# An attention and mixture-of-experts kernel: weighted values divided straight out of PSUM, gathers that add, a band mask moved to GpSimd for some steps

## What is computed

```python
xn = layernorm(x)
# attention: 32 heads of 8 channels; query i sees keys i-8 .. i+7
attn = (q @ k.T) * 8 ** -0.5
attn = where(m != 0, attn * m, -inf)      # m falls off with |i - j| / 16
s = softmax(attn) @ v @ proj_w.T + proj_b
# feed-forward: one of 8 experts per token (argmax of the router), and a shared expert
out[t] = (silu(xs @ gate_w[e]) * (xs @ up_w[e])) @ down_w[e]      # xs = xn * sigmoid(max logit)
shared = (silu(xn @ shared_gate_w) * (xn @ shared_up_w)) @ shared_down_w
g = silu(out + shared)
result = x + s * g
```

## Time and profile before

| | |
|---|---|
| Time before, median of 3 runs | 634.32 us (633.57 to 634.75) |
| The profiled execution's own time | 633.25 us |
| Its span in the profile | 631.4 us |
| TensorE busy | 557.1 us (88%) |
| VectorE busy | 403.7 us (64%) |
| ScalarE busy | 307.9 us (49%) |
| GpSimd busy | 187.0 us (30%) |

### The profile page before, as it was taken

The page is one execution under the profiler, slowest core; times in us unless marked ns, Lnnn a source line. Parts: engine busy times, 40 slices in busy tenths (PEclk is TensorE's granted clock), DMA queues, the critical chain, the costliest instruction groups (busy, mean ns, idle before and its releaser), DMA issues. The chain is left out here.

```text
span 631.4 us, 10599 instructions
## 1 busy us (share of the span) xinstructions
PE 557.1 (88%) x3358; PEld 479.0 (76%) x3358; DVE 403.7 (64%) x853; ACT 307.9 (49%) x762; POOL 187.0 (30%) x160
## 2 busy tenths in 40 slices
PE   1979999979889999999999999999886877769865
PEld 1757898758768999888999888898675655657754
DVE  6766556885756446456446456446688888886873
ACT  1473654458673644533634533645454533636331
POOL 6001011148861111000111000114655545532230
PEclk9989999979999999999999999999989899999997
DMA  8525441113327576576577566443133333331110
GB/s 292 180 70 174 151 141 55 49 49 99 113 92 216 163 223 202 167 203 199 143 218 208 168 203 190 126 129 115 50 110 110 108 99 101 117 102 26 35 42 17
DMA packets 107371, 82.89 MB, mean 131 GB/s; under 512 B 42293, under 2 KB 104757, under 8 KB 107317
## 3 DMA queue, kind: packets, MB, share of 16 engines
q1 hardware_dynamic: 98628, 68.72, 36.9%
q0 software_dynamic: 3072, 8.39, 4.2%
q10 hardware_dynamic: 5616, 5.11, 2.3%
HBM read 59.12 MB, written 23.07 MB: 130 GB/s over the span
## 5 line engine op out<-in xcount | busy, mean ns | idle before, releaser
L427 POOL TENSOR_TENSOR Sx<-Sx,mx 128x752 f32<-128x752 f32 x64 | 93.7, 1465 | 407.1 <-DVE mx L729 406.5
L945 PE MATMUL psV<-VB,PTs 128*128 128x132 f32 x1024 | 133.1, 282 | 30.2 <-ACT Or L470 29.7
L945 PEld LDWEIGHTS psV<-VB,PTs 128*128 128x128 f32 x1024 | 127.1, 193 | 36.1 <-issue 34.9
L470 ACT ACTIVATE Or<-psV 32x128 f32<-32x128 f32 x256 | 68.5, 268 | 150.5 <-DVE rs L759 146.2
L920 PE MATMUL psS<-kBD,qBD 128*128 128x188 f32 x512 | 104.0, 327 | 0.0
L920 PEld LDWEIGHTS psS<-kBD,qBD 128*128 128x128 f32 x512 | 86.9, 193 | 10.4 <-issue 2.2
L751 DVE STREAM_TRANSPOSE PTs<-Sx 128x512 f32<-128x512 f32 x128 | 82.9, 685 | 1.0 <-ACT Sx L500 1.0
L995 PE MATMUL psM<-xT,EB 128*128 128x128 f32 x624 | 76.4, 276 | 0.0
L995 PEld LDWEIGHTS psM<-xT,EB 128*128 128x128 f32 x624 | 73.8, 192 | 2.1 <-ACT qBD L489 1.3
L722 DVE TENSOR_TENSOR Sx<-psS,cst 128x752 f32<-128x752 f32 x64 | 59.6, 932 | 24.5 <-PE psS L920 24.5
L736 DVE SCALAR_TENSOR_TENSOR ea<-et,psM 128x256 f32<-128x256 f32 x39 | 16.4, 421 | 76.3 <-PE psM L995 47.2
(11 more groups left out here) (107 smaller groups left out, 689.3 us busy)
## 6 DMA issues: line engine op xcount, KB each, us to landing
EB<-in_L_ffn_gate_w SPq DMA_DIRECT2D x39, 256.0 KB, 2.9
EB<-in_L_ffn_up_w SPq DMA_DIRECT2D x39, 256.0 KB, 3.6
EB<-in_L_ffn_down_w SPq DMA_DIRECT2D x39, 256.0 KB, 3.1
VB<-v_dram SPq DMA_DIRECT2D x256, 32.0 KB
stage<-xs_dram SPq DMA_DIRECT2D x39, 128.0 KB, 2.2
ys_dram<-yb ACTq DMA_DIRECT2D x39, 128.0 KB, 3.1
xs_dram<-blank SPq DMA_DIRECT2D x9, 512.0 KB, 3.8
v_dram<-vS SPq DMA_DIRECT2D x8, 512.0 KB, 2.9
```

Source lines behind the costliest of these rows:

```text
L427: nc.gpsimd.tensor_tensor(s, s, mx[n % 3][:, :].unsqueeze(2).broadcast_to([P, 2 * G, KW]), ALU.subtract).then_inc(a_sub, 1)
L470: return nc.scalar.activation(dst, src, ACT.Copy)
L945: last = mm(psV[:, j, at:at + HS * VW], PTs[n % 2][:, k, j, i, :], VB[n % 2][:, i, k, :, VW * j:VW * j + VW], start=k == 0, stop=k == 1)
```

## The change

1. **Divide out of PSUM.** `o_out`, the tile Or and the semaphore `a_O` go. `divide(n)` becomes four VectorE instructions, one for each 32 partitions, that read psV and the reciprocals and write O. `weighted(n)` waits for `divide(n-1)` (`a_nrm`). `divide` and `turned` stand right after `invert`, ahead of the second expert tile and of the shared expert.
2. **Gathers that add.** `combine`, its semaphore `d_z` and the use of Y as landing buffer go. `gather(c)` is an indirect DMA with an add into the shared output's own rows. It is issued in the step before part c's silu, after `subtract` of that step, and first waits for the shared output (`f_sh`). ScalarE's `silu(c)` waits for the landing and, for part 3 on, for VectorE's silu three parts earlier.
3. **Masking on GpSimd.** In steps 0 to 7 and 18 to 37 (28 of 64), TensorE leaves out the two mask matmuls; GpSimd's new `banded(n)` adds the fp32 mask to Sx after `weigh(n)`, and `largest(n)` waits for it. In these steps `largest(n)` stands behind `normalise(n+1)` and `flipped(n-1)`. The constants that are loaded first grow by 12 x 47 columns (from 435 to 999 a partition).

```diff
+C_BAND = C_HEAD + HS
+C_STAY = C_BAND + 12 * KW
...
+def masked_late(n):
+    return n < BATCH or E0 <= n < E0 + NP
...
-        Or = sb("Or", [P, KC, 2, HS, HD])
...
+            def banded(n):
+                pool.wait_ge(a_mul, n + 1)
+                s = Sx[n % 3][:, :, :].rearrange("p (m r) k -> p m r k", r=HS)[:, :, :, 0:KW]
+                kind = 2 * KC * mask_kind(n)
+                nc.gpsimd.tensor_tensor(s, s, band[:, kind:kind + 2 * KC, :].unsqueeze(2).broadcast_to([P, 2 * KC, HS, KW]),
+                                        ALU.add).then_inc(a_add, 1)
...
             def gather(c):
...
-                if c >= 3:
-                    pool.wait_ge(d_w, c - 2)
+                pool.wait_ge(f_sh, c + 1)
                 for k in range(CT):
                     t = c * CT + k
-                    pool.indirect_dma_start(Y[b][:, k * C:(k + 1) * C], None, ys_dram,
-                                            bass.IndirectOffsetOnAxis(ap=slot[:, t:t + 1], axis=0)).then_inc(d_y[b], 16)
-
-            def combine(c):
...
-                nc.gpsimd.tensor_tensor(z, Y[b], z, ALU.add).then_inc(d_z, 1)
+                    pool.indirect_dma_start(shared_rows(c * CT)[:, k, :], None, ys_dram,
+                                            bass.IndirectOffsetOnAxis(ap=slot[:, t:t + 1], axis=0),
+                                            compute_op=ALU.add).then_inc(d_y[c % 3], 16)
 
             for n in range(LAST + 1):
-                for c in silu_at(n):
-                    combine(c)
                 if n < U:
+                    if masked_late(n):
+                        banded(n)
                     subtract(n)
...
-                if n == C_STEP:
-                    for c in range(3):
-                        gather(c)
-                for c in silu_at(n - 1):
-                    if c + 3 < NC:
-                        gather(c + 3)
+                for c in silu_at(n + 1):
+                    gather(c)
...
             def silu(c):
-                act.wait_ge(d_z, c + 1)
+                act.wait_ge(d_y[c % 3], 16 * CT * (c // 3 + 1))
+                if c >= 3:
+                    act.wait_ge(d_w, c - 2)
...
             def largest(n):
-                dve.wait_ge(a_mul, n + 1)
+                if masked_late(n):
+                    dve.wait_ge(a_add, len([k for k in range(n + 1) if masked_late(k)]))
+                else:
+                    dve.wait_ge(a_mul, n + 1)
...
             def divide(n):
                 dve.wait_ge(a_rec, n + 1)
-                dve.wait_ge(a_O, n + 1)
...
+                for h in range(HS):
+                    rows = slice(QB * h, QB * h + QB)
+                    last = tt(o[rows], v[rows, :, :, HD * h:HD * h + HD],
+                              inverse[rows].unsqueeze(3).broadcast_to([QB, KC, 8, HD]), ALU.mult)
+                last.then_inc(a_nrm, 1)
...
                 for j in range(KC):
-                    mm(psS[:, j, 0:BW], identb[:, :], maskb[:, kind:kind + 2, :, :].rearrange("p i r k -> p (i r k)"),
-                       start=True, stop=False)
+                    if not late:
+                        mm(psS[:, j, 0:BW], identb[:, :], maskb[:, kind:kind + 2, :, :].rearrange("p i r k -> p (i r k)"),
+                           start=True, stop=False)
```

More of the change, by code:

```diff
@@ L240, in build @@
         m_full = [sem(f"m_full{i}") for i in range(MB)]
-        a_qk, a_S, a_mul, a_max, a_sub, a_exp, a_PT, a_V, a_PV, a_O, a_rec, a_nrm, a_OT, a_s = (
-            sem("a_" + n) for n in ("qk", "S", "mul", "max", "sub", "exp", "PT", "V", "PV", "O", "rec", "nrm", "OT", "s"))
+        a_qk, a_S, a_mul, a_add, a_max, a_sub, a_exp, a_PT, a_V, a_PV, a_rec, a_nrm, a_OT, a_s = (
+            sem("a_" + n) for n in ("qk", "S", "mul", "add", "max", "sub", "exp", "PT", "V", "PV", "rec", "nrm", "OT", "s"))
         x_v, x_vd = ([sem(f"x_{n}{i}") for i in range(2)] for n in ("v", "vd"))
@@ L248, in build @@
         d_y, d_x, d_st = ([sem(f"d_{n}{i}") for i in range(3)] for n in ("y", "x", "st"))
-        d_z, d_t, d_w, d_g, d_o = (sem("d_" + n) for n in ("z", "t", "w", "g", "o"))
+        d_t, d_w, d_g, d_o = (sem("d_" + n) for n in ("t", "w", "g", "o"))
         x_tiles = x.rearrange("(t p) c -> p t c", p=P)
@@ L500, in exps @@
                 nc.scalar.activation(s, s, ACT.Exp).then_inc(a_exp, 1)
[L502 to L511, removed]
             def v_out(t):
@@ L763, in divide @@
                 dve.wait_ge(a_rec, n + 1)
[L764 removed]
                 if n >= 1:
                     dve.wait_ge(a_OT, n)
[L767 to L769 removed]
+                v = psV[:, :, 1:1 + 2 * HS * VW].rearrange("p j (i c) -> p j i c", c=VW)
+                inverse = rs[n % 2][:, :, :, :].rearrange("p j i s -> p j (i s)")
+                o = O[:, :, :, :, :].rearrange("p j i s d -> p j (i s) d")
+                for h in range(HS):
[3 more added lines that the diff above has]
+                last.then_inc(a_nrm, 1)
             def turned(n):
@@ L826, in _ @@
                     weigh(n)
-                    largest(n)
+                    if not masked_late(n):
+                        largest(n)
                 if n == 0:
@@ L842, in _ @@
                     flipped(n - 1)
+                if n < U and masked_late(n):
+                    largest(n)
                 for i in pair_at(n, 1)[:1]:
@@ L847, in _ @@
                     invert(n - 2)
+                    divide(n - 2)
+                    turned(n - 2)
                 for i in pair_at(n, 1)[1:]:
@@ L907, in scores @@
                 h, u = divmod(n, UH)
-                if n == 0:
+                late = masked_late(n)
+                if n == BATCH:
                     pe.wait_ge(s_cast, 2)
@@ L920, in scores @@
                         last = mm(psS[:, j, i * HS * KW:(i + 1) * HS * KW], qBD[h % 2][:, j, k, :, :].rearrange("p s q -> p (s q)"),
-                                  kBD[h % 2][:, j, :, k * QB:k * QB + KW], start=False, stop=i == 1)
+                                  kBD[h % 2][:, j, :, k * QB:k * QB + KW], start=late, stop=late or i == 1)
                 last.then_inc(a_S, 1)
@@ L939, in weighted @@
                 if n >= 1:
-                    pe.wait_ge(a_O, n)
+                    pe.wait_ge(a_nrm, n)
                 for j in range(KC):
```

13 lines of the change are left out of this document (2 added, 11 removed).

## The result

The changed kernel takes 614.76 us (612.71 to 615.40), against 634.27 for the kernel before: a ratio of 0.969, with an interval from 0.967 to 0.971. Forecast were 605 and a range of 594 to 618: faster, inside the range, 9.8 us slower than the likeliest case. The profiled execution took 614.93, its span 613.1.

What follows compares the result with a forecast made beforehand. TensorE was taken to bound steps 0 to 7 and 19 to 38, GpSimd's scatters 8 to 18, no single engine 41 to 54. 633.25 +1 -3 -0 -6.4 -0.7 -16 -2 -2 = 604.2, median 605, range 594 to 618.

Steps and rivals of the forecast that it cites:

- Constants: Before the first step: loading 564 more columns ahead of the weights costs 1 us (0 to 3.3).
- Steps 0 to 7: First stage: masks off TensorE save 2.6 us, with ScalarE's dropped `o_out` 3 in all (1 to 5).
- Steps 8 to 38: Scatters keep steps 8 to 18 unchanged; 20 masked steps in 18 to 37 save 0.32 us each, 6.4.
- `banded`: GpSimd's mask add takes 1.45 us; `largest` waits about 0.2 us for it, over 0.3 a step would be wrong.
- The divide: VectorE's four divides out of PSUM take 0.8 us together; a step with the hole before them gains 0.7.
- No combine: `result`'s first multiply falls to 0.68 us without GpSimd's `combine` beside it: 1.3 less in odd steps, 0.9 in even.
- Steps 41 to 54: VectorE needs 97 us, plus 0.55 a step for two near engines: 105 us, 16 less (10 to 24).
- Steps 55 to 62: Stage before the drain, TensorE near full: 2 us less (0 to 4).
- half the gain: Steps 41 to 54: divide costs 1.6 us or TensorE's bursts keep holes open, 8 of 16 lost; 615 us, chance 0.17.
- Masks don't pay: Masked stages: `banded` lengthens a chain TensorE awaits or collides with `normalise`, 9.4 us lost; 614 us, chance 0.10.
- all in balance: Steps 41 to 54 take 97 us instead of 105, first stage gains 5, steps 55 to 62 gain 3; 594 us, chance 0.12.
- The adding gather is slow: Steps 41 to 54: landings from 5.9 us after issue lengthen steps; at 12.1 us, 648 us in all; chance 0.06.

Runs made afterwards that it cites:

- early gathers: The changed kernel with the gathers of parts 0 to 11 issued two steps ahead of their silu instead of one: 604.45 us, ratio 0.953.
- silu last: The changed kernel with ScalarE's tanh of a part moved to the end of its step, gathers left where the change puts them: 604.49 us, ratio 0.953.

## Why the prediction came out as it did

The sign and the range held. In the terms of the profiled execution 604.2 were forecast and 614.93 came: of these 10.7 us, 5.6 lie in steps 41 to 54, 4.3 in steps 55 to 62, 1.9 in the drain and 0.4 in steps 39 and 40; the start gives 1.3 back (the rest is rounding and 0.1 from the other stages).

- **Constants.** Forecast +1, measured -0.3 (the first `weigh` at 27.21 instead of 27.53). 0.32 of this are the two mask matmuls that step 0 leaves out ahead of it, so the longer constants cost nothing that shows.
- **Steps 0 to 7.** Forecast -3, measured -2.8, of which the masks alone give 2.6.
- **Steps 8 to 38.** Forecast -6.4, all of it in steps 19 to 38; measured -6.7, but split otherwise: the windows give -2.4 for steps 8 to 18 (81.06 against 83.50) and -4.2 for 19 to 38 (227.80 against 232.02, forecast 225.6). In steps 20 to 37 most steps are 0.32 shorter, as forecast, and together they are 5.4 shorter (5.7 with the masks alone). Step 19 is 1.2 longer: the expert tiles start sooner and then wait for their weights, which no term held:

```profile
190.09 2.02 PE L996 MATMUL psM<-xT,EB 128*128 128x128 f32 x16 [1.63 <-DMA EB<-in_L_ffn_up_w]
```

For the 2.4 before it nothing was forecast; the divide alone gives 3.1 in steps 8 to 18 and loses 2.1 of it again in step 19, the masks alone give nothing there.
- **`banded`.** 1.68 us instead of 1.45. VectorE waited 11.7 us for it in 21 waits, 0.56 each where 0.2 was said and 0.3 was the sign of an error. That sign came up falsely: with the masks alone 8.9 us were gained, so the wait cost nothing that shows, as TensorE stayed full (226.96 of 227.80).
- **The divide.** Four of 0.287 and 1.19 together; the forecast was 0.8, and the term mis-sized is the overlap: 0.09 each was taken over from the reciprocals, and these four start 0.30 apart. The estimate of 1.03 by the Trainium skill, page VectorE: DVE Perf Modes, section The TRN2 errata, without overlap, was nearer, and still 0.16 low. From the reciprocals' end to the divide's end 1.23 us pass instead of 1.52 (in the drain 596.38 to 597.61): the hole went, and VectorE's own work filled most of it. A step with a hole gained 0.3 there and not 0.7. So VectorE's busy time came to 450.6 us and not to 425: the divides take 73.5 where the old ones took 23.5, 50 us more, and 64 x 0.5 = 32 had been said; another 7.6 are left open.
- **Steps 39 and 40, the drain.** Forecast -0.7 and -2, measured -0.3 and -0.1. In the drain the chain runs through psV, and psV is free no sooner: from the reciprocals' end of the drain's first pass TensorE restarts after 1.29 us before (614.61 to 615.90) and 1.37 after:

```profile
596.14 0.24 DVE L752 RECIPROCAL rs<-psV 128x8 f32<-128x8 f32 x2
596.42 1.19 DVE L764 TENSOR_TENSOR O<-psV,rs 32x128 f32<-32x128 f32 x4
...
597.75 3.67 PE L946 MATMUL psV<-VB,PTs 128*128 128x132 f32 x16 [6.96 <-DVE O L764]
```
- **No combine.** L804, the multiply that was L807, is 0.684 us in the mean over all 14, as forecast. The collision was GpSimd's `combine`: it is gone where only the gather is changed (0.683) and there where `combine` is kept (0.68 to 2.31 with the divide alone, 1.359 in the mean with the masks alone). The Trainium skill, page SBUF — State Buffer, section Who interferes with whom, agrees, for instructions of VectorE with two SBUF inputs beside one of GpSimd that reads SBUF; of those with one input it excepts the modes that use both of VectorE's ports, which the prediction left out. Step 45 takes 6.86 (forecast 6.4, and 6.8 with a divide of 1.19).
- **Steps 41 to 54.** Forecast -16 to 105, measured -10.4 to 110.7. **The step that failed** is in the adding gather: "`silu` on ScalarE now holds up what is queued behind it [...] those wait for TensorE work that ends later", and "hidden". The landing itself was sized rightly, 2 to 4 us behind the second issue (2.8 in the timeline of step 48, from 480.59). The issues were not: 1.55 to 2.01 us each on GpSimd where I had the gather's 0.95, so that they end 7.0 to 7.45 us after `weigh` and not 5.8, and ScalarE's tanh began mostly 1.3 to 3.5 us into the next step, not 0.9. And the q projections behind it had long been ready: the queue's order was not compared with when each piece of its work would be ready. That early gathers (same order, landings early up to step 52) and silu last (landings as late, other order) each bring 604.5 shows this to be the loss. The sign "no ScalarE wait of more than 1 us outside the last parts" failed as well: nine of the ten waits in steps 43 to 52 are 1.8 to 5.9 us long, though of these steps only 48 is longer than with early gathers. In steps 53 and 54, where the gather itself was held up, VectorE waits 2.64 and 2.30 us for the silu, and TensorE stands: for 3.02 us up to 532.13, after which the clock falls, and 16 matmuls take 3.86 us at a granted clock of 0.50.

```profile
535.79 3.86 PE L946 MATMUL psV<-VB,PTs 128*128 128x132 f32 x16 [0.99 <-DVE O L764]
537.70 0.63 ACT L546 ACTIVATE EB<-xnT 128x512 f32<-128x512 f32 x1 [5.91 <-DMA xnT<-ys_dram,slot]
538.37 0.69 DVE L797 SCALAR_TENSOR_TENSOR xnT<-EB,xnT 128x512 f32<-128x512 f32 x1 [2.30 <-ACT EB L546]
```

```profile
517.70:527.00 9.30, 7.67 (x49) 6.60 (x48) 8.24 (x20) 4.43 (x9) 4.57 (x3) 1.00 0.54 126
527.00:537.30 10.30, 6.29 (x32) 5.21 (x32) 6.70 (x14) 3.39 (x7) 4.58 (x3) 0.78 0.46 102
```
- **Steps 55 to 62.** Forecast -2, measured +2.3, +0.5 with early gathers, -0.5 with silu last. Step 62 has the wait for a landing again, 5.35 us, and takes 9.05 (before 7.56, with silu last 7.99). Step 56 takes 8.25 (before 7.48, with early gathers 6.57): TensorE's q projections ahead of it take 3.13 us, at a granted clock of 0.60, where early gathers show 1.89 at 1.00.

```profile
541.94 0.33 PE L917 MATMUL psS<-maskb,identb 128*128 128x376 bf16 x1 [2.29 <-DVE Sx L712]
...
543.99 3.13 PE L896 MATMUL psM<-xnT,wqkv 128*128 128x256 f32 x8
```

With the queue mended the kernel stands at 604.5, which is the 605 of the forecast, and partly by offset: VectorE's work was put 0.4 us a step too low (the divide), and the 0.55 us a step added for two engines near to each other was hardly needed.

Of the rivals, "half the gain" named 615 for another reason (a divide of 1.6 us, or open holes), so its number is no proof of it. "Masks don't pay" is out, since the masks alone give 8.9, and "all in balance" with its 97 us for steps 41 to 54. "The adding gather is slow" named a chain through the landing from 5.9 us on; the landings stay under it, and yet the gather alone makes the kernel 6.8 us slower, by the queue behind the wait and not by that chain.

The three parts alone give -4.3, +6.8 and -8.9 us, together -6.4; all at once they give -19.5. The missing 13 are the pairing of the first two, though no run has these two alone. The steps tell it: in steps 41 to 62 the parts alone give -1.0, +7.1 and 0, and all at once -8.1, so that the whole difference lies where the masks change nothing. The divide takes ScalarE's psV copies out from behind the wait (bringing them back cost 14.2 us, 11.4 of it in these steps), and the gather takes `combine` away, on which the divide's gain was spent. How the 13 divide between the two is not shown.

## What to carry to other kernels

When a transfer takes over an engine's work, write down who waits for its landing, and for each piece of work behind that wait the time at which it would have been ready: waits of up to 6.0 us at the end of a queue cost next to nothing here, and waits of up to 6.2 us in its middle cost 10 us in all. Ask too whether the next transfer needs something from behind the wait. An edit that only moves work from a second engine to the bounding one, as the divide does, gains by what it unties: price it together with the other edits of its queue, not as a hole closed. Do not take an overlap from another shape; count starts.

## What the runs showed of the hardware

- VectorE's 32-partition instructions out of PSUM with 128 elements take 0.287 us and start 0.30 apart, with 64 elements 0.215 and about 0.18: halving the size saves 0.12 of 0.30.
- An indirect DMA that adds takes GpSimd 1.55 us and up to 2.01 to issue, against 0.95 without the add; from issue to landing 3.7 to 5.1 us for 128 rows of 1 KB. GpSimd's DMA queue carries 6144 packets where it had carried 3072, for the same 8.39 MB; from step 40 on, where the gathers are, 4608 for 1536.
- VectorE's plain add of two SBUF operands stands still beside GpSimd's add as its fused multiply does (1.97 us for 0.69).
- GpSimd's mask add on 128 x 752 took 1.68 us in the mean, its subtraction of the same size 1.48.
